# Values turned around: v stationary, probabilities divided before their turn

## The reference

```
xn = layernorm(x) * gamma
q  = xn @ w_q            # 16 heads of 64
k, v = split(xn @ w_kv)  # 16 heads of 64
k, v = [2 null keys, k], [2 null values, v]
q, k = l2norm(q), l2norm(k)        # times q_scale, k_scale
sim  = 8 * q @ k^T + ALiBi bias, causal mask
out  = softmax(sim) @ v            # per head, 258 keys
x    = x + concat(out) @ w_out     # 1024 -> 128
```

## Time and profile before

| | |
|---|---|
| Median of three runs | 655.25 us |
| Profiled execution | 660.73 us, span 658.9 us |
| TensorE matmuls | 573.4 us busy (87%), 3792 |
| TensorE weight loads | 453.3 us (69%) |
| VectorE | 421.6 us (64%) |
| ScalarE | 430.3 us (65%) |
| GpSimd | 356.6 us (54%) |
| Mean granted TensorE clock | 0.981 |
| Chain of waits | TensorE 59%, VectorE 15%, GpSimd 11%, issue 9%, ScalarE 3% |

### The profile page before, as it was taken

How to read it: one execution, slowest core, us unless ns; L and a number is a source line. 1 busy time by engine, 2 the same in 40 slices (tenths; PEclk the granted TensorE clock), 3 DMA queues, 4 the chain that set the end, 5 groups by cost and what they waited for, 6 DMA issues and landing times.

```text
span 658.9 us, 13422 instructions
## 1 busy us (share of the span) xinstructions
PE 573.4 (87%) x3792; PEld 453.3 (69%) x3792; DVE 421.6 (64%) x1523; ACT 430.3 (65%) x1197; POOL 356.6 (54%) x310
## 2 busy tenths in 40 slices
PE   2446979987899989888999999999999999998787
PEld 1444768875567767766777777777877777777566
DVE  5773836455688676889655665665656566577653
ACT  2712857535677787766577777767767776877562
POOL 3618845033888697444275544544455433688830
PEclk9999979999699999999999999999999999999899
DMA  9502223140110013000000000011001100111100
GB/s 317 197 4 53 70 68 74 49 152 16 27 32 25 18 33 97 1 1 2 1 24 23 25 22 23 27 29 21 21 27 29 25 14 10 29 48 49 53 21 9
DMA packets 26326, 29.13 MB, mean 44 GB/s; under 512 B 3920, under 2 KB 22384, under 8 KB 25744
## 3 DMA queue, kind: packets, MB, share of 16 engines
q1 hardware_dynamic: 21680, 18.89, 8.9%
q0 software_dynamic: 4576, 9.38, 6.2%
HBM read 19.94 MB, written 8.32 MB: 43 GB/s over the span
## 4 chain that ended last, share of the span: by engine, by line
PE 59%; DVE 15%; POOL 11%; issue 9%; ACT 3%; DMA 1%; another core or an unknown queue 1%; SPq 0%; POOLq 0%; DVEq 0%; ACTq 0%
PE b_last L1816 8%; PE b_upB L1801 7%; POOL taken L622 5%; PE b_rest L1865 4%; PE b_upB L1787 4%; PE b_last L1679 3%; POOL rn L571 3%; PE b_rest L1654 3%; PE b_rest L1613 2%; PE b_upA L1472 2%; PE b_upA L1734 2%; PE b_last L1472 2%; PE b_rest L1836 2%; PE b_upA L1474 2%; PE b_upA L1473 2%
## 5 line engine op out<-in xcount | busy, mean ns | idle before, releaser
L868 ACT ACTIVATE prb<-prb,mneg 128x130 f32<-128x130 f32 (+1 forms) x256 | 114.8, 450 | 93.9 <-DVE mneg L1415 89.4
L571 POOL TENSOR_TENSOR rn<-ss,halves 128x8 f32<-128x8 f32 x64 | 107.6, 1681 | 102.0 <-DVE ss L1353 101.3
L1415 DVE CUSTOM_DVE_ANT_0 prb<-b_upB,bias 128x130 f32<-128x130 f32 (+1 forms) x256 | 82.1, 356 | 122.1 <-PE b_upB L1801 117.5
L499 POOL DMA_INDIRECT moe_buf<-normal_rows,source x79 | 78.8, 997 | 103.1 <-PE b_rest L1768 63.5
L1816 PEld LDWEIGHTS b_last<-v,prT_all 128*128 128x128 f32 x768 | 100.0, 192 | 12.6 <-DVE qs_all L1401 4.8
L1816 PE MATMUL b_last<-v,prT_all 128*128 128x64 f32 x768 | 101.4, 268 | 3.0 <-DVE qs_all L1401 2.4
L1801 PE MATMUL b_upB<-qkT 64*128 64x258 f32 (+1 forms) x512 | 77.7, 381 | 0.0
L877 ACT ACTIVATE prT_all<-b_rest 128x512 f32<-128x512 f32 (+1 forms) x128 | 61.5, 480 | 10.9 <-PE b_rest L1865 7.8
L1865 PE MATMUL b_rest<-cst,prb 128*128 128x128 f32 x384 | 63.6, 275 | 0.0
L314 POOL TENSOR_TENSOR qk<-qk,rn 128x512 f32<-128x512 f32 x56 | 59.1, 1055 | 4.4
L1865 PEld LDWEIGHTS b_rest<-cst,prb 128*128 128x128 f32 x384 | 47.6, 150 | 18.0 <-issue 17.8
(11 more groups left out here) (325 smaller groups left out, 1294.2 us busy)
## 6 DMA issues: line engine op xcount, KB each, us to landing
expert_rows<-moe_buf SPq DMA_DIRECT2D x20, 128.0 KB
expert_rows<-moe_buf SPq DMA_DIRECT2D x39, 64.0 KB
bias<-w_up SPq DMA_DIRECT2D x1, 2048.0 KB, 8.9
down<-w_dn SPq DMA_DIRECT2D x2, 1024.0 KB, 10.0
moe_buf<-w_up SPq DMA_DIRECT2D x4, 512.0 KB, 3.9
moe_buf<-normal_rows,source POOLq DMA_INDIRECT x79
qk<-x SPq DMA_DIRECT2D x8, 128.0 KB, 4.0
v<-w_qk SPq DMA_DIRECT2D x1, 1024.0 KB, 11.5
```

The source lines that it names most:

```text
L499: nc.gpsimd.indirect_dma_start(out=room, out_offset=None, in_=normal_rows[layer], in_offset=bass.IndirectOffsetOnAxis(ap=source[layer][:, ...
L571: nc.gpsimd.tensor_tensor(rn[hs], ss[hs], halves[:], ALU.pow).then_inc(pool_root, 1)
L868: nc.scalar.activation(prb[k % 3][:, i, 0:n], prb[k % 3][:, i, 0:n], ACT.Exp, scale=-1.0, bias=mneg[:, qt, h:h + 1], accum_out=lsum[:, qt, ...
L1415: nc.vector.tensor_tensor_reduce(prb[k % 3][:, i, 0:n], b_sim[i][:, 0:n], bias[:, h, KEYS - n:KEYS], 1.0, FMAX, ALU.add, ALU.min, mneg[:, ...
```

## The change

The matmul of the values takes v as the stationary operand (64 columns, one head) and the turned probabilities as the moving one (128 columns). The two heads of an item write the lower and the upper 64 partitions of `b_pv`, which now holds channels x tokens, four pairs of heads side by side. That is the layout in which the projection with w_out needs it, so the four turns of a quad and their buffer `o_half` go, and `b_pv` is copied to `oT` directly. Since the tokens are no longer on the partitions, the division by the sums moves ahead of the turn: one step after the scores, VectorE takes the reciprocals of the item's two sums and multiplies the probabilities of head 0, GpSimd those of head 1. The turn of the probabilities, their copies and the values come one step later (2, 2 and 4 steps after the scores), and so do the null keys' copies and turns. The null values become four matmuls with `nvbd` stationary. GpSimd's gathers for batches 2 to 7 are spread over three steps instead of coming in one. Declarations of semaphores and the added name `shares` at the head of GpSimd's list are left out below; `turned_outputs` (L1451 to L1457) is removed.

```diff
@@ -525,7 +525,7 @@
-            def take_rows(b):
+            def take_rows(b, parts=range(2 * T)):
@@ -581,14 +581,25 @@
                     row_roots(1)
-                if s % 3 == 0 and 0 <= s < 3 * (B - 2):
-                    take_rows(s // 3 + 2)
+                for b in range(2, B):
+                    parts = [n for n in range(2 * T) if s == 3 * (b - 2) + 2 * n // 3]
+                    if parts:
+                        take_rows(b, parts)
...
+
+            def shares(s):
+                for k in step_at(s, 1):
+                    qt, hp = divmod(k % STEPS, HP)
+                    n, h = NULL + P * (qt + 1), 2 * hp + 1
+                    pool.wait_ge(dve_rl, k + 1)
+                    pool.wait_ge(act_exp, 2 * k + 2)
+                    mine = prb[k % 3][:, 1, 0:n]
+                    nc.gpsimd.tensor_tensor(mine, mine, rl[:, qt, h:h + 1].to_broadcast([P, n]), ALU.mult).then_inc(pool_share, 1)
@@ -869,7 +880,7 @@
             def values(s):
-                for k in step_at(s, 1):
+                for k in step_at(s, 2):
@@ -1388,18 +1399,12 @@
             def scores(s):
-                for m in quad_at(s, 7):
-
-                    tile, first = m // 2 % T, m % 2 * HALF
-                    dve.wait_ge(act_exp, 8 * m + 8)
-                    heads8 = rl[:, tile, first:first + HALF]
-                    nc.vector.reciprocal(heads8, lsum[:, tile, first:first + HALF]).then_inc(dve_rl, 1)
-                    dve.wait_ge(dve_rl, m + 1)
+                for m in quad_at(s, 8):
...
                     dve.wait_ge(pe_pvn, m + 1)
-                    if m >= 2:
-                        dve.wait_ge(pe_oT, m - 1)
-                    nc.vector.tensor_tensor(o_half[m % 2].rearrange("p (h d) -> p h d", h=HALF), b_pv.rearrange("p (h d) -> p h d", h=HALF),
-                                            heads8.unsqueeze(2).to_broadcast([P, HALF, DH1]), ALU.mult).then_inc(dve_norm, 1)
+                    if m:
+                        dve.wait_ge(pe_op, m)
+                    nc.vector.tensor_copy(oT[:].rearrange("p a q -> p (a q)"), b_pv).then_inc(dve_oT, 1)
@@ -1410,12 +1415,22 @@
                             dve.wait_ge(pe_prT, k - 2)
+                            dve.wait_ge(dve_null, k - 2)
...
                                                        ALU.add, ALU.min, mneg[:, qt, h:h + 1]).then_inc(dve_sim, 1)
-                for m in quad_at(s, 5):
+                for k in step_at(s, 1):
+
+                    qt, hp = divmod(k % STEPS, HP)
+                    n, h = NULL + P * (qt + 1), 2 * hp
+                    dve.wait_ge(act_exp, 2 * k + 2)
+                    nc.vector.reciprocal(rl[:, qt, h:h + 2], lsum[:, qt, h:h + 2]).then_inc(dve_rl, 1)
+                    dve.wait_ge(dve_rl, k + 1)
+                    mine = prb[k % 3][:, 0, 0:n]
+                    nc.vector.tensor_scalar(mine, mine, rl[:, qt, h:h + 1], None, ALU.mult).then_inc(dve_share, 1)
+                for m in quad_at(s, 6):
@@ -1436,10 +1451,11 @@
                     nc.vector.tensor_tensor(acc_all[:, i], b_op, acc_all[:, i], ALU.add).then_inc(dve_add, 1)
-                for k in step_at(s, 1):
+                for k in step_at(s, 2):
...
                     m, at = k // 4, k % 4 * 2 * NULL
-                    dve.wait_ge(act_exp, 2 * k + 2)
+                    dve.wait_ge(dve_share, k + 1)
+                    dve.wait_ge(pool_share, k + 1)
@@ -1684,7 +1692,7 @@
                     if b:
-                        pe.wait_ge(act_prT, s - 1)
+                        pe.wait_ge(act_prT, s - 2)
@@ -1763,12 +1771,11 @@
                     pe.wait_ge(rows_loaded[i % 4], PAIRS_LOADED + 16 * (i // 4 + 1))
-                    pe.wait_ge(dve_oT, s // 4 - 1)
...
             def scores(s):
-                for m in quad_at(s, 5):
+                for m in quad_at(s, 6):
@@ -1795,46 +1802,39 @@
                             pe.wait_ge(dve_sim, 2 * k - 1 + i)
-                        for m in quad_at(k - 1, 10) if i else quad_at(k - 1, 5):
+                        for m in quad_at(k - 1, 10) if i else quad_at(k - 1, 6):
...
             def values(s):
-                for k in step_at(s, 3):
+                for k in step_at(s, 4):
...
                         if k:
-                            pe.wait_ge(dve_norm, k // 4)
+                            pe.wait_ge(dve_oT, k // 4)
...
-                    for i in range(2):
-                        h = 2 * (p % HP) + i
-                        at = (k % 4 * 2 + i) * DH1
-                        for c in range(p // HP + 1):
-                            ins = nc.tensor.matmul(b_pv[:, at:at + DH1], prT[k % 3][:, i, c * P:(c + 1) * P], v[:, c, h * DH1:(h + 1) * DH1],
-                                                   start=(k % 4 == 0 and i == 0 and c == 0), stop=False, skip_group_check=True)
+                    at = k % 4 * P
+                    for c in range(p // HP + 1):
+                        for i in range(2):
+                            h = 2 * (p % HP) + i
+                            ins = nc.tensor.matmul(b_pv[i * DH1:(i + 1) * DH1, at:at + P], v[:, c, h * DH1:(h + 1) * DH1],
+                                                   prT[k % 3][:, i, c * P:(c + 1) * P], start=(k % 4 == 0 and c == 0), stop=False,
+                                                   skip_group_check=True)
                     ins.then_inc(pe_pv, 1)
-                for m in quad_at(s, 6):
+                for m in quad_at(s, 7):
...
                     pe.wait_ge(dve_pnT, m + 1)
-                    nc.tensor.matmul(b_pv, pnT[:], nvbd[:, m % 2], start=False, stop=True, skip_group_check=True).then_inc(pe_pvn, 1)
+                    for a in range(4):
+                        ins = nc.tensor.matmul(b_pv[:, a * P:(a + 1) * P], nvbd[:, m % 2, a * P:(a + 1) * P], pnT[:], start=False, stop=(a == 3),
+                                               skip_group_check=True)
+                    ins.then_inc(pe_pvn, 1)
...
             def shared_bank(s):
-                for m in quad_at(s, 8):
-
-                    pe.wait_ge(dve_norm, m + 1)
-                    pe.wait_ge(act_v, min(m + 2, 4 * B))
-                    if m:
-                        pe.wait_ge(dve_oT, m)
-                    if tiles_before(s):
-                        pe.wait_ge(tile_dve["xl"], tiles_before(s))
-                    for i in range(4):
-                        ins = nc.tensor.transpose(b_y[:, i * P:(i + 1) * P], o_half[m % 2][:, i * P:(i + 1) * P], ident)
-                    ins.then_inc(pe_oT, 1)
@@ -1842,15 +1842,13 @@
                         pe.wait_ge(wv_in, 16)
-                    if m >= 2:
-                        pe.wait_ge(dve_oT, m - 1)
...
             def turned_values(s):
-                for k in step_at(s, 1):
+                for k in step_at(s, 2):
@@ -1859,7 +1857,8 @@
                         pe.wait_ge(act_xaT, 1)
-                    pe.wait_ge(act_exp, 2 * k + 2)
+                    pe.wait_ge(dve_share, k + 1)
+                    pe.wait_ge(pool_share, k + 1)
```

30 lines of the change are left out of this document (12 added, 18 removed).

## The result

The changed kernel takes 735.78 us (median of 4 runs, 729.46 to 739.56), the kernel before beside it 653.67: a ratio of 1.124, with an interval of 1.115 to 1.134. The forecast was 680 us, +25; +82 came. The profiled execution took 739.56 us, its span is 737.7. The chips differ ahead of step 0: its first scores start at about 160 us in some traces and at 168 to 173 us in others, whatever the kernel. The trace of before is one of the late ones (169.9), that of the change is not (159.8), so the steps have lost 10 us more than the two spans (658.9 and 737.7) differ by.

A forecast was written before the change was run, and what follows sets the result against it. It took TensorE, VectorE or GpSimd as the bound, depending on the stretch. Terms of -3.6 + 8.4 + 5 + 3 + 12 = +25 us on the median of 655.25 gave 680 us, range 648 to 709.

The forecast's parts named there:

- What bounds the kernel: Before the change: TensorE in steps 48 to 95, VectorE in 32 to 47, GpSimd in 0 to 16 and 105 to 121.
- dense expert-tile steps: 27 of steps 48 to 102: TensorE's expert matmul waits for VectorE's delayed gate, 0.31 us each, +8.4 us (2 to 14).
- steps 0 to 19: GpSimd gets 8 us of multiplies beside 10 us of idle time, gathers no longer four at a time: +3 us.
- 20 to 47: VectorE's net addition of 9.8 us in these steps, counted half: +5 us (0 to 10).
- TensorE, -3.6 us: Steps 0 to 102: dropped turns save slightly more than array-shape switches and null values cost, -0.035 us a step.
- Rival 1: The two heads' halves of the values do not run together on TensorE: +29 us, 709 us; chance 0.14.
- VectorE's block, 0.75 us: Added reciprocal and multiply per step, with the copy behind held by GpSimd's multiply: 0.75 us (0.4 to 0.85).
- The tail, +12 us: Last steps, paced by GpSimd: its lost head start of 4.2 us and 14 multiplies of 8.0 us, +12 us (7 to 15).
- 2: Only the last steps on GpSimd cost; VectorE's added work fits its idle time: +8, 664 us; chance 0.24.
- 3: TensorE's array-shape switches are not paid, loads and passes overlap: faster, about 636 us; chance 0.13.

## Why the prediction was wrong, step by step

- **What bounds the kernel**: right for before. The step that failed stands behind it: I priced each addition by its length on the engine that gets it, and let the others be bound as before. In the change no engine is the bound. The terms that this left too small are "dense expert-tile steps" (+8.4, measured 32.2) and "steps 0 to 19" with "20 to 47" (+8, measured 39.7); the clock had no term.
- **TensorE, -3.6 us**: right in sign, too small. Concurrent halves (0.109 a pair) and the 0.09 on the way in are as taken; the load on the way out is hidden. The mean of the block's differences is (0.68 - 0.84 + 0.46 - 0.405) / 2 = -0.05 a step, forecast +0.045, and the kernel without division is 11 us faster than before, the null turns, the output's turns and VectorE's part of them and of the division included. Rival 1 is wrong. A change of the array's shape costs 0.09 us of empty TensorE here as in the earlier trace rows. The Trainium skill's rule (TensorEngine Tiling (Array Packing), Key Properties), that a change of the tiling mode drains TensorE and that different tiles may load and multiply in parallel, agrees with both measurements.
- **VectorE's block, 0.75 us**: right in size, for another reason, and that is luck. Reciprocal and multiply run 0.16 + 0.685 for 258 columns and 0.16 + 0.497 for 130, a mean of 0.75; the null copy behind them costs no more than before, apart from its wait for GpSimd (15.8 us in nine waits). I had the multiply at 0.42 and 0.29 and the copy held. Unheld it takes 0.36 and 0.29 (the medians without GpSimd's), and it is the multiply that is held. My upper bound of 0.85 was that of 130 columns alone; with my own terms 258 columns give 0.20 + 0.42 + 0.60 = 1.22. GpSimd's own lengths (0.60 and 0.35 forecast, 0.633 and 0.407 measured) were near. The rule of the Trainium skill that I had weighed (GPSIMD Engine Reference, Key points: SBUF interfaces shared with VectorE) agrees, and reaches the multiply itself, where I had applied it to the copy. It does not do so in every step: some multiplies take the shortest time in the change too.
- **Dense expert-tile steps, +8.4 us**: the mechanism failed and not only the size, 32.2 us in steps 48 to 95. The wait that I priced, of the expert matmul for the gate, should have come in most of 27 steps; it is 4.2 us in six waits (L1480 for L1382). I looked only at the gate's slack (L1472) and never at the v projection, which waits in the same steps for the low part behind the same block: 22.8 us in 13 waits. Without GpSimd's multiply the stretch takes 215.6 us, 12.0 above before, which is near my 8.4; the low part first takes 207.7 even with GpSimd's multiply.
- **The clock**: no step of mine, no rival, no bound. The trace of before showed 1.00 in the stretches in which TensorE is dense, and 0.93 in steps 0 to 16, where it idles; I read both and drew nothing from them. It is worth 11.5 us in steps 48 to 95. In the rest it was not isolated. It also makes a wait cost by jumps: without GpSimd's multiply the wait ahead of the v projection is still 18.3 us in 13 waits, the longest 2.0 us, but the clock of steps 48 to 95 is 0.99.
- **Steps 0 to 19, +3, and 20 to 47, +5**: 39.7 us came in steps 0 to 47. I counted GpSimd's multiplies against its idle time. That idle time is of no use to an engine that stands at a wait with its gathers behind it: a multiply with hardly any length costs nearly as much there (132.4 us in steps 0 to 31) as one of full length (139.9), and with none they take 106.6. The +5 stood for VectorE's added work: without GpSimd's multiply steps 0 to 47 take 166.4 us, 166.3 before and 158.4 with no division at all, so VectorE's part costs 8 us there, which the layout gives back.
- **The tail, +12 us**: right, also in its mechanism. Between the gathers of steps 105 and 107 lie now 646.04 - 636.98 = 9.06 us (7.80), forecast near 8.9, without a gap above 0.3 us on GpSimd. The gather of step 105 starts 3.0 us behind the scores (forecast 2.3; before, 1.9 ahead of them). Steps 96 to 127 lost 17.1 us, of which 12.2 go with GpSimd's multiply.
- **Rivals**: 2 and 3 fell with the +82. That it went wrong on the side of rival 1, through none of its mechanism, is why the range did not hold it: every end of it was a sum of lengths, and no case had a new wait between two engines that both stood on the third.

The gather and the multiply after it in the tail:

```profile
636.98 1.05 POOL L633 DMA_INDIRECT taken<-expert_rows,pos  x1 [0.16 <-issue]
...
644.70 1.19 POOL L602 TENSOR_TENSOR prb<-prb,rl 128x258 f32<-128x258 f32 x2
646.04 1.04 POOL L633 DMA_INDIRECT taken<-expert_rows,pos  x1 [0.16 <-issue]
```

What stays open: how much of its bound of 36 us the clock costs in steps 0 to 47, where 0.73 to 0.88 was granted (no filler was tried there); what the spread gathers do to the ring; and which of the two, VectorE held or GpSimd busy longer, makes the 0.04 of the multiply's length. A GpSimd multiply that nobody waits for would tell; it was not tried.

## What to carry to other kernels

Before work goes to an idle engine, list what stands behind it in that engine's order and who waits for that: an operation with a wait costs by its place, here more than by its length. For each instruction that is lengthened, list all who wait for anything later on the same engine, not the consumer that comes to mind, and put first what the bound engine waits for. When TensorE starts to idle, count the slower clock that can follow as well; and of several engines with room, take the one whose order already runs beside the data, as ScalarE's here.

## What the runs showed of the hardware

- Two f32 matmuls of 64 output partitions each, in different halves of the columns, start 7 ns apart and run together: from one pair to the next 0.109 us, behind the first pair 0.160.
- A VectorE multiply (tensor_scalar, 258 columns) beside a GpSimd multiply of 258 columns takes 685 ns in the mean and 811 in the median, without it 485 and 357; the shortest is 355 in both kernels.
- Filling idle TensorE with 14 useless turns at each of 13 waits made the kernel faster (1.124 to 1.112), and the passes of the v projections there, up to 1,194 ns in the change, then took at most 697; the clock of steps 48 to 95 went from 0.95 to 1.00.
